# Head attention: the values matmuls of a key tile in one piece of 512 columns instead of two of 256, and another order of the matmuls around them

## The chip, the cores and the metric

One core of a Trainium2 chip runs the kernel. The metric is the device time of one execution in microseconds, taken as the median of several runs; the profile is of one further execution. TensorE (PE) does matmuls, with its weight loads shown apart as PEld; VectorE (DVE), ScalarE (ACT) and GpSimd (POOL) do the rest; SyncE (SP) issues DMAs.

## The reference, cut to what matters

The program is four layers on x of shape (2, 2048, 256): agent attention, a transformer block with a mixture of experts, a selective scan and an FP4 feed-forward. The change lies in the 16-head attention of the second layer:

```python
q = (src @ Wq + bq).reshape(B, T, NHEAD, HEAD_DIM)      # B, T = 2, 2048; 16 heads of 16
k = (src @ Wk + bk).reshape(B, T, NHEAD, HEAD_DIM)
v = (src @ Wv + bv).reshape(B, T, NHEAD, HEAD_DIM)
scores = jnp.einsum('bqhd,bkhd->bhqk', q, k) * scale
probs = jax.nn.softmax(scores, axis=-1)
out = jnp.einsum('bhqk,bkhd->bqhd', probs, v).reshape(B, T, d)
```

## The kernel before

The function `head_attention` treats four heads (a quad) and 512 queries (`GN`) as one step. There are 2 batches x 4 quads x 4 query chunks = 32 steps (`STEPS`), and each step goes over 16 key tiles of 128 keys (`KT`), so there are 512 iterations (st, kt). In each iteration TensorE has three kinds of work, and the names below are used from here on:

- **First pass** (`first_pass`, L977): four matmuls of 48 rows x 512 columns, x = 0 to 3, which give the logits of queries against keys for the row maxima. Matmuls 0 and 2 use the array's rows 0 to 63, matmuls 1 and 3 rows 64 to 127. Each writes one PSUM bank of `ps_m`, and there are three such banks (`BANKS`), taken in the fixed turn of `BankPlan`. VectorE reduces each bank to its maximum (`maxima_of`, L921), in the same order. `bank_free` makes each first-pass matmul wait until the reduce of the one three places earlier in the turn is over. The first pass runs 21 units ahead of the rest (`ahead`: one step and `LEAD` = 5).
- **Scores** (`scores`, L992): for each of two pairs of heads, two matmuls of 50 rows x 512 columns, one for each half of the array's rows, into `ps_s[pair]`. ScalarE turns them to `probs` with an Exp (`exps`, L876), 128 x 1024 each.
- **Values** (`values`, L1004): for each of four heads, probs times v into 32 partitions of `ps_o`. Each uses 128 rows and 32 columns of the array, so that the four lie side by side in it. The matmul is fp32 and is profiled as two instructions.

ScalarE's `exps(n, 0)` waits until the values of tile n - 2 are done (`pv_done`), because `probs` has room for two tiles; the scores of a pair wait until that pair's last Exp is done.

In iteration kt the order on TensorE is now: values of tile kt - 1 for the first 256 query columns; first pass 0 and 1; scores of kt + 1, pair 0; values of kt - 1 for the last 256 columns; first pass 2 and 3; scores of kt + 1, pair 1. At the end of iteration 1, `turn_out` (L1013) transposes the last step's output, and at the end of iteration 11 (`LEAD_SHIFT`) `turn_shift` (L983) transposes the next step's maxima; each takes one place in the turn of the three banks, and ScalarE copies it out (L887; L895 and L896). VectorE reduces the maxima of a step to one shift at L928.

Of the kernel before, what the change touches and what calls it, by code (L numbers as in the profile page):

```python
# [26 lines left out]
GN = GT * P  # L27
# [431 lines left out]
VW = 32  # L459
# [213 lines left out]
QC = L // GN  # L673
KT = L // P
NQ = B * QUADS
STEPS = NQ * QC
# [39 lines left out]
def ahead(st, kt):  # L716

    return (st + 1, kt + LEAD) if kt + LEAD < UNITS else (st + 2, kt + LEAD - UNITS)
# [5 lines left out]
def unit_of(i):  # L724

    return i // 8, i % 8 // 2, i % 2 * 2


def head_attention(nc, scratch, ident):
# [6 lines left out]
    with ExitStack() as ctx:  # L736
        r = Room(nc, ctx, "att")
        qs, ks = r.sb("qs", [P, 2, QC, PAIRS, GN], F32R), r.sb("ks", [P, 2, PAIRS, L], F32R)
        vs = [r.sb(f"vs{i}", [P, KT, QH * VW]) for i in range(2)]
# [4 lines left out]
        probs = r.sb("probs", [P, 4, 2, GN])  # L744
# [5 lines left out]
        ps_o = r.ps("ps_o", [P, GN])  # L750
# [5 lines left out]
        shifted, exp_done, pv_done = r.sem("shifted"), r.sem("exp_done"), r.sem("pv_done")  # L756
# [8 lines left out]
        def rows_of(e, first, n):  # L765
            return slice(e * ROW_TILE + first, e * ROW_TILE + first + n)

        with nc.Block() as block:
# [185 lines left out]
            @block.tensor  # L954
            def _(pe):

                def bank_free(key):

                    last = plan.before(key)
                    if last is None:  # L960
                        return
                    if last[0] == "shift":
                        pe.wait_ge(m_copied, 2 * (last[1] + 1))
                    elif last[0] == "out":
                        pe.wait_ge(o_t_ready, last[1] + 1)
                    else:
                        pe.wait_ge(maxed, plan.reduced[last])

                def first_pass(s, i, x):

                    key = ("m", s, i, x)
                    p, t, chunk = unit_of(i)
                    own, c = rows_of(x % 2, 0, TERMS), chunk + x // 2
                    if i == 0 and x == 0 and s % QC == 0 and s > 0:
                        pe.wait_ge(quad_loaded, s // QC * LOADS)
                    bank_free(key)
                    pe.matmul(ps_m[plan.bank(key)][:, :], qs[own, s // QC % 2, s % QC, p, t * P:(t + 1) * P],  # L977
                              ks[own, s // QC % 2, p, c * GN:(c + 1) * GN], start=True, stop=True).then_inc(scored, 1)

                def turn_shift(s):  # L980
                    bank_free(("shift", s))
                    pe.wait_ge(m_ready, s + 1)
                    pe.transpose(ps_m[plan.bank(("shift", s))][0:QT, 0:P], m_neg[:, :], ident[:, :]).then_inc(m_turned, 1)  # L983

                def scores(st, kt, pair):
                    n = st * KT + kt
                    if kt == 0 and pair == 0:
                        pe.wait_ge(shift_loaded, (st + 1) * SHIFTS)
                    if n > 0:
                        pe.wait_ge(exp_done, 2 * (n - 1) + pair + 1)  # L990
                    for e in range(2):
                        mm = pe.matmul(ps_s[pair][:, e, :], ks[rows_of(e, 0, ROWS), st // QC % 2, pair, kt * P:(kt + 1) * P],  # L992
                                       qs[rows_of(e, 0, ROWS), st // QC % 2, st % QC, pair, :], start=True, stop=True)
                    mm.then_inc(shifted, 1)

                def values(st, kt, half):

                    n = st * KT + kt
                    cols = slice(half * (GN // 2), (half + 1) * (GN // 2))
                    pe.wait_ge(exp_done, 2 * (n + 1))  # L1000
                    if kt == 0 and half == 0 and st > 0:
                        pe.wait_ge(o_copied, st)
                    for h in range(QH):
                        mm = pe.matmul(ps_o[h * VW:(h + 1) * VW, cols], vs[st // QC % 2][:, kt, h * VW:(h + 1) * VW],  # L1004
                                       probs[:, (2 * n + h // 2) % 4, h % 2, cols], start=(kt, half) == (0, 0), stop=(kt, half) == (KT - 1, 1))
                    if half == 1:
                        mm.then_inc(pv_done, 1)

                def turn_out(st):
                    bank_free(("out", st))  # L1010
                    pe.wait_ge(o_copied, st + 1)
                    for t in range(GT):
                        mm = pe.transpose(ps_m[plan.bank(("out", st))][:, t * P:(t + 1) * P], o_sb[:, t * P:(t + 1) * P], ident[:, :])  # L1013
                    mm.then_inc(o_turned, 1)

                for i in range(UNITS):
                    if i % (UNITS // 2) == 0:
                        for h in (2 * i // UNITS * 2, 2 * i // UNITS * 2 + 1):
                            pe.wait_ge(first_loaded[h], (HEAD_LOADS + (h == QH - 1)) * 16)
                    for x in range(4):  # L1020
                        first_pass(0, i, x)
                turn_shift(0)
                for i in range(LEAD):
                    for x in range(4):
                        first_pass(1, i, x)
                pe.wait_ge(ones_laid, 4 * PAIRS * 16)
                def next_scores(st, kt, pair):
                    if kt + 1 < KT:
                        scores(st, kt + 1, pair)
                    elif st + 1 < STEPS:  # L1030
                        scores(st + 1, 0, pair)

                def last_values(st, kt, half):
                    if kt > 0:
                        values(st, kt - 1, half)
                    elif st > 0:
                        values(st - 1, KT - 1, half)

                scores(0, 0, 0)
                scores(0, 0, 1)  # L1040
                for st in range(STEPS):
                    for kt in range(KT):
                        s, i = ahead(st, kt)
                        last_values(st, kt, 0)
                        if s < STEPS:
                            first_pass(s, i, 0)
                            first_pass(s, i, 1)
                        next_scores(st, kt, 0)
                        last_values(st, kt, 1)
                        if s < STEPS:  # L1050
                            first_pass(s, i, 2)
                            first_pass(s, i, 3)
                        next_scores(st, kt, 1)
                        if st > 0 and kt == 1:
                            turn_out(st - 1)
                        if st + 1 < STEPS and kt == LEAD_SHIFT:
                            turn_shift(st + 1)
                for half in range(2):
                    values(STEPS - 1, KT - 1, half)
                turn_out(STEPS - 1)  # L1060


# [1861 lines left out]
```

## Time and profile before

| | us |
|---|---|
| median of 3 runs | 3895.88 (3894.23 to 3899.1) |
| the profiled execution | 3899.1 |
| its span in the trace | 3897.4 |
| head attention's main loop, within the span | about 300 to 1640 |

The page's busy shares of the whole span are PE 85%, PEld 49%, DVE 75%, ACT 52% and POOL 30%. They mix all layers; for this change only the stretch from about 300 to 1640 us counts. A timeline row gives the start, the time from the start of the first to the end of the last instruction of a merged group, the engine, the line, the operation and the count. A matmul's row starts with its weight load when the array is not at work for it, and starts later where the load went ahead.

### The profile page before, as it was taken

Reading aid. Unit: us, or ns where it says so; the run is one execution under the profiler, and the core shown is the slowest. Engines: PE = TensorE matmul, PEld = TensorE weight load, DVE = VectorE, ACT = ScalarE, POOL = GpSimd, SP = SyncE. Lnnn points to the kernel's source line nnn. Section 1 sums busy time; section 2 is a strip of 40 time slices with the busy share of each in tenths; the row PEclk is TensorE's granted clock in tenths of the full one; section 3 lists DMA queues with packets and bytes.
Section 4 is the critical chain, followed back from the end, with each engine's and each line's share of the span. In section 5 each row is a group of like instructions: output and inputs, shape, how many; then the busy total and the mean of one; then the engine's idle time right before and its main releaser. Section 6 shows DMA issues by size and latency. Waiting matters only on the chain. (4 is left out here: it accounts for less than half of the span.)

```text
span 3897.4 us, 87366 instructions
## 1 busy us (share of the span) xinstructions
PE 3311.1 (85%) x34938; PEld 1906.6 (49%) x34939; DVE 2921.1 (75%) x4552; ACT 2033.6 (52%) x2900; POOL 1184.2 (30%) x928
## 2 busy tenths in 40 slices
PE   4769999999999999875999749984989898847876
PEld 1433333333333333254666433333867677636665
DVE  5659999999999999334444346773879798758986
ACT  0316777777777777721111255664454564325553
POOL 0100000000000000015000730002889899847775
PEclk8868999999999999966999759997999999979998
DMA  1664123030321300152221442334333333221110
GB/s 54 224 175 46 19 34 48 5 49 5 48 32 21 47 6 5 29 186 96 66 65 60 126 158 92 127 122 131 98 114 108 121 107 108 80 73 54 57 33 19
DMA packets 231409, 296.89 MB, mean 76 GB/s; under 512 B 51577, under 2 KB 166530, under 8 KB 229378
## 3 DMA queue, kind: packets, MB, share of 16 engines
q1 hardware_dynamic: 213794, 258.22, 24.2%
q0 software_dynamic: 6144, 17.05, 1.3%
q10 hardware_dynamic: 11120, 16.62, 1.2%
q8 instruction: 260, 4.26, 0.5%
q14 instruction: 91, 0.75, 0.1%
HBM read 174.75 MB, written 116.47 MB: 75 GB/s over the span
## 5 line engine op out<-in xcount | busy, mean ns | idle before, releaser
L921 DVE TENSOR_REDUCE att_maxima<-att_ps_m 128x1 f32<-128x512 f32 x2048 | 1285.6, 684 | 80.1 <-PE att_ps_m L977 78.3
L876 ACT ACTIVATE att_probs<-att_ps_s 128x1024 f32<-128x1024 f32 x1024 | 999.3, 1021 | 280.8 <-PE att_ps_o L1004 268.2
L1004 PE MATMUL att_ps_o<-att_probs,att_vs 128*32 128x256 f32 x8192 | 657.0, 393 | 4.9 <-ACT att_probs L876 0.6
L2220 POOL TENSOR_TENSOR ss_ch<-ss_h,ss_c_rep 128x1024 f32<-128x1024 f32 x256 | 602.3, 2390 | 86.8 <-DVE ss_h L2298 86.7
L977 PE MATMUL att_ps_m<-att_ks,att_qs 48*128 48x512 f32 x2048 | 584.1, 511 | 29.9 <-DMA att_ks<-scratch_k 29.2
L2328 PE MATMUL ss_ps_u<-ss_diag,ss_dx_t 128*32 128x128 f32 x16384 | 493.5, 279 | 86.3 <-DVE ss_h L2298 49.7
L2328 PEld LDWEIGHTS ss_ps_u<-ss_diag,ss_dx_t 128*32 128x32 f32 x16384 | 467.5, 113 | 146.6 <-issue 91.1
L977 PEld LDWEIGHTS att_ps_m<-att_ks,att_qs 48*128 48x128 f32 x2048 | 238.3, 188 | 472.6 <-DVE att_maxima L921 389.4
L2252 ACT ACTIVATE ss_decay<-ss_delta,ss_a_neg 128x1024 f32<-128x1024 f32 x256 | 292.0, 1146 | 335.7 <-DVE ss_h L2298 178.1
L992 PE MATMUL att_ps_s<-att_qs,att_ks 50*128 50x512 f32 x2048 | 453.8, 404 | 3.6 <-DMA att_qs<-att_m_parts 0.8
L2298 DVE TENSOR_TENSOR_SCAN ss_h<-ss_decay,ss_ps_u 128x1024 f32<-128x1024 f32 x128 | 283.8, 2270 | 96.2 <-PE ss_ps_u L2328 54.1
L1004 PEld LDWEIGHTS att_ps_o<-att_probs,att_vs 128*32 128x32 f32 x8192 | 162.5, 108 | 360.9 <-issue 339.6
L2298 DVE TENSOR_TENSOR_SCAN ss_h<-ss_decay,ss_carry,ss_ps_u 128x1024 f32<-128x1024 f32 x128 | 291.0, 2328 | 48.2 <-ACT ss_decay L2252 20.8
L992 PEld LDWEIGHTS att_ps_s<-att_qs,att_ks 50*128 50x128 f32 x2048 | 222.5, 188 | 24.7 <-ACT att_probs L876 20.8
L856 POOL TENSOR_TENSOR att_heads<-att_o_t,att_sums 128x256 f32<-128x256 f32 x32 | 19.8, 619 | 692.9 <-DVE att_sums L936 692.9
L849 POOL TENSOR_TENSOR att_m_parts<-att_m_t,att_m_parts 16x128 fp32r<-16x128 f32 x32 | 14.4, 449 | 680.3 <-ACT att_m_parts L896 680.3
L1457 ACT ACTIVATE ex_y<-ex_ps_y,ex_x 128x256 f32<-128x256 f32 x72 | 34.1, 473 | 301.7 <-PE ex_ps_y L1528 301.7
L1661 POOL DMA_INDIRECT mo_back<-scratch_sorted_y,moe_packed x64 | 61.1, 954 | 345.5 <-DMA mo_b_norm<-in_b_norm 318.7
L2035 PE MATMUL si_ps_xz<-si_xn_t,si_w_in 128*128 128x512 f32 x256 | 119.5, 622 | 35.1 <-ACT si_xp L1983 15.8
L2207 POOL TENSOR_SCALAR_AFFINE_SELECT ss_diag<-ss_b_t 128x512 f32<-128x512 f32 x64 | 40.4, 642 | 339.7 <-DMA ss_b_t<-scratch_b_t 339.7
L1510 PE MATMUL ex_ps_h<-moe_w_w,ex_x_t 128*128 x288 | 137.2, 599 | 0.4 <-issue 0.4
L1528 PE MATMUL ex_ps_y<-moe_w_w,ex_hid_t 128*128 x576 | 136.1, 379 | 0.0
(391 smaller groups left out, 4570.0 us busy)
## 6 DMA issues: line engine op xcount, KB each, us to landing
ss_delta<-scratch_delta SPq DMA_DIRECT2D x64, 512.0 KB
att_qs<-scratch_q SPq DMA_DIRECT2D x96, 128.0 KB, 9.3
att_ks<-scratch_k SPq DMA_DIRECT2D x96, 128.0 KB, 10.7
ex_x<-scratch_sorted_x SPq DMA_DIRECT2D x72, 132.0 KB, 2.1
scratch_sorted_y<-ex_y SPq DMA_DIRECT2D x72, 128.0 KB, 1.7
scratch_v<-qkv_v_ext SPq DMA_DIRECT2D x8, 1024.0 KB
scratch_q<-qkv_parts SPq DMA_DIRECT2D x16, 512.0 KB, 5.3
scratch_k<-qkv_parts SPq DMA_DIRECT2D x16, 512.0 KB, 6.0
```

What stands on the lines that cost most here:

```text
L876: act.activation(probs[:, (2 * n + pair) % 4, :, :], ps_s[pair][:, :, :], ACT.Exp, scale=HD ** -0.5).then_inc(exp_done, 1)
L921: dve.tensor_reduce(maxima[:, j, at:at + 1], ps_m[plan.bank(key)][:, :], AX.X, ALU.max).then_inc(maxed, 1)
L977: pe.matmul(ps_m[plan.bank(key)][:, :], qs[own, s // QC % 2, s % QC, p, t * P:(t + 1) * P], ks[own, s // QC % 2, p, c * GN:(c + 1) * GN], ...
L992: mm = pe.matmul(ps_s[pair][:, e, :], ks[rows_of(e, 0, ROWS), st // QC % 2, pair, kt * P:(kt + 1) * P], qs[rows_of(e, 0, ROWS), st // QC % ...
L1004: mm = pe.matmul(ps_o[h * VW:(h + 1) * VW, cols], vs[st // QC % 2][:, kt, h * VW:(h + 1) * VW], probs[:, (2 * n + h // 2) % 4, h % 2, cols ...
L1510: mm = pe.matmul(ps_h[slot][:, :], x_t[:, slot, k, :], w1[:, bass.ds(e, 1), k, :].rearrange("p a f -> p (a f)"), start=k == 0, stop=k == K ...
L1528: mm = pe.matmul(ps_y[slot][:, 0, :], hid_t[:, slot, f, :], w2[:, bass.ds(e, 1), f, :].rearrange("p a c -> p (a c)"), start=f == 0, stop=f ...
L2035: mm = pe.matmul(ps_xz[n % XZ][:, :], w_in[:, k, n * P:(n + 1) * P], xn_t[:, slot, k, :], start=k == 0, stop=k == KC - 1)
L2220: pool.tensor_tensor(ch[:, w.n % (CH_GROUPS * DQ), :], h[:, w.n % H_SLOTS, :], c_rep[:, w.ng, :], ALU.mult).then_inc(s["ch_ready"], 1)
L2252: act.activation(decay[:, w.n % DECAYS, :], delta[:, w.delta % DELTAS, :], ACT.Exp, scale=a_neg[:, at:at + 1]).then_inc(s["decay_ready"], 1)
L2298: dve.tensor_tensor_scan(h[:, w.n % H_SLOTS, :], decay[:, w.n % DECAYS, :], ps_u[w.n % U_BANKS][:, :], start, ALU.mult, ALU.add).then_inc( ...
L2328: mm = pe.matmul(ps_u[w.n % U_BANKS][q * DSUB:(q + 1) * DSUB, j * P:(j + 1) * P], dx_t[:, w.part % 2, j, w.dq * DSUB:(w.dq + 1) * DSUB], d ...
```

## The change

`values` loses its argument `half`: one matmul for each head covers all 512 query columns. The lag and lead of the work are expressed as before (values of the last tile, scores of the next), but the order changes. In iteration kt it is now: first pass 0; scores of **kt**, pair 1; first pass 1; values of kt - 1, all columns; first pass 2 and 3; scores of kt + 1, pair 0. The order of the first-pass matmuls in the turn of the banks, and everything on the other engines, stay as they are.

```diff
-                def values(st, kt, half):
+                def values(st, kt):
                     n = st * KT + kt
-                    cols = slice(half * (GN // 2), (half + 1) * (GN // 2))
                     pe.wait_ge(exp_done, 2 * (n + 1))
-                    if kt == 0 and half == 0 and st > 0:
+                    if kt == 0 and st > 0:
                         pe.wait_ge(o_copied, st)
                     for h in range(QH):
-                        mm = pe.matmul(ps_o[h * VW:(h + 1) * VW, cols], vs[st // QC % 2][:, kt, h * VW:(h + 1) * VW],
-                                       probs[:, (2 * n + h // 2) % 4, h % 2, cols], start=(kt, half) == (0, 0), stop=(kt, half) == (KT - 1, 1))
-                    if half == 1:
-                        mm.then_inc(pv_done, 1)
+                        mm = pe.matmul(ps_o[h * VW:(h + 1) * VW, :], vs[st // QC % 2][:, kt, h * VW:(h + 1) * VW],
+                                       probs[:, (2 * n + h // 2) % 4, h % 2, :], start=kt == 0, stop=kt == KT - 1)
+                    mm.then_inc(pv_done, 1)
...
                 scores(0, 0, 0)
-                scores(0, 0, 1)
                 for st in range(STEPS):
                     for kt in range(KT):
                         s, i = ahead(st, kt)
-                        last_values(st, kt, 0)
                         if s < STEPS:
                             first_pass(s, i, 0)
+                        scores(st, kt, 1)
+                        if s < STEPS:
                             first_pass(s, i, 1)
-                        next_scores(st, kt, 0)
-                        last_values(st, kt, 1)
+                        if kt > 0:
+                            values(st, kt - 1)
+                        elif st > 0:
+                            values(st - 1, KT - 1)
                         if s < STEPS:
                             first_pass(s, i, 2)
                             first_pass(s, i, 3)
-                        next_scores(st, kt, 1)
+                        if kt + 1 < KT:
+                            scores(st, kt + 1, 0)
+                        elif st + 1 < STEPS:
+                            scores(st + 1, 0, 0)
```

## Rows read from the trace of the kernel before

**Rows 1.** The page, costliest groups: line, engine, names and shapes, busy and mean, idle before

```profile
L921 DVE TENSOR_REDUCE att_maxima<-att_ps_m 128x1 f32<-128x512 f32 x2048 | 1285.6, 684 | 80.1 <-PE att_ps_m L977 78.3
L876 ACT ACTIVATE att_probs<-att_ps_s 128x1024 f32<-128x1024 f32 x1024 | 999.3, 1021 | 280.8 <-PE att_ps_o L1004 268.2
L1004 PE MATMUL att_ps_o<-att_probs,att_vs 128*32 128x256 f32 x8192 | 657.0, 393 | 4.9 <-ACT att_probs L876 0.6
```

**Rows 2.** Windows by stretch: busy us (count) of PE, PEld, DVE, ACT, POOL; clock

```profile
304.40:317.40 13.00, 13.00 (x78) 4.23 (x80) 7.70 (x13) 6.24 (x7) 0.00 (x0) 0.50 1.07 128
...
1592.00:1640.00 48.00, 44.44 (x441) 15.30 (x437) 2.57 (x6) 42.03 (x46) 1.07 (x2) 1.00 0.02 4
1000.00:1200.00 200.00, 199.33 (x1861) 77.48 (x1858) 193.33 (x316) 155.39 (x173) 4.89 (x10) 1.00 0.22 34
```

**Rows 3.** Timeline of two iterations in the steady loop

```profile
1000.39 0.64 PE L1004 MATMUL att_ps_o<-att_probs,att_vs 128*32 128x256 f32 x8
...
1002.90 0.64 PE L1004 MATMUL att_ps_o<-att_probs,att_vs 128*32 128x256 f32 x8
1003.47 0.21 PEld L977 LDWEIGHTS att_ps_m<-att_ks,att_qs 48*128 48x128 f32 x2 [0.41 <-DVE att_maxima L921]
1003.47 0.52 PE L977 MATMUL att_ps_m<-att_ks,att_qs 48*128 48x512 f32 x2
...
1003.81 0.41 PE L992 MATMUL att_ps_s<-att_qs,att_ks 50*128 50x512 f32 x2
1004.15 0.16 PEld L1004 LDWEIGHTS att_ps_o<-att_probs,att_vs 128*32 128x32 f32 x8 [0.36 <-issue]
1004.15 0.64 PE L1004 MATMUL att_ps_o<-att_probs,att_vs 128*32 128x256 f32 x8
...
1005.42 0.64 PE L1004 MATMUL att_ps_o<-att_probs,att_vs 128*32 128x256 f32 x8
```

**Rows 4.** Timeline of VectorE alone, the first step's maxima, ahead of the loop

```profile
259.71 28.78 DVE L921 TENSOR_REDUCE att_maxima<-att_ps_m 128x1 f32<-128x512 f32 x48
```

**Rows 5.** Timeline where VectorE had been idle before a reduce

```profile
1011.87 0.50 PE L977 MATMUL att_ps_m<-att_ks,att_qs 48*128 48x512 f32 x2
...
1012.40 1.29 DVE L921 TENSOR_REDUCE att_maxima<-att_ps_m 128x1 f32<-128x512 f32 x2 [0.29 <-PE att_ps_m L977]
...
1013.11 0.54 PE L977 MATMUL att_ps_m<-att_ks,att_qs 48*128 48x512 f32 x2
```

**Rows 6.** Timelines at 1.2 GHz, cut to single instructions

```profile
301.43 0.62 PE L992 MATMUL att_ps_s<-att_qs,att_ks 50*128 50x512 f32 x1
301.50 0.98 PE L977 MATMUL att_ps_m<-att_ks,att_qs 48*128 48x512 f32 x2
...
308.70 1.08 PE L1004 MATMUL att_ps_o<-att_probs,att_vs 128*32 128x256 f32 x8
310.87 0.65 PE L1004 MATMUL att_ps_o<-att_probs,att_vs 128*32 128x256 f32 x4
```

**Rows 7.** Timeline around the next step's shift

```profile
1007.85 0.22 DVE L928 TENSOR_REDUCE att_m_neg<-att_maxima 128x16 f32<-128x64 f32 x1
...
1008.10 2.48 DVE L921 TENSOR_REDUCE att_maxima<-att_ps_m 128x1 f32<-128x512 f32 x4
...
1009.52 0.28 PE L983 MATMUL att_ps_m<-all_ident,att_m_neg 128*16 128x128 f32 x1
```

**Rows 8.** The line of the shift's reduce: duration, first and last start

```profile
L928 DVE TENSOR_REDUCE att_m_neg<-att_maxima x32: 219/220/220, 288.5 to 1594.1; 128x16 f32<-128x64 f32 x32
```

**Rows 9.** Timeline around the transposes of a step's output

```profile
1024.27 0.40 PE L1004 MATMUL att_ps_o<-att_probs,att_vs 128*32 128x256 f32 x4
...
1024.60 0.53 PE L977 MATMUL att_ps_m<-att_ks,att_qs 48*128 48x512 f32 x2
...
1024.94 0.42 PE L992 MATMUL att_ps_s<-att_qs,att_ks 50*128 50x512 f32 x2
...
1025.29 0.66 PE L1013 MATMUL att_ps_m<-all_ident,att_o_sb 128*128 128x128 f32 x4
1025.87 0.16 PEld L1004 LDWEIGHTS att_ps_o<-att_probs,att_vs 128*32 128x32 f32 x8 [0.17 <-ACT att_probs L876]
```

**Rows 10.** Timeline of the last iterations, which have no first pass

```profile
1619.82 0.49 PE L992 MATMUL att_ps_s<-att_qs,att_ks 50*128 50x512 f32 x2
1619.96 1.94 ACT L876 ACTIVATE att_probs<-att_ps_s 128x1024 f32<-128x1024 f32 x2 [0.27 <-PE att_ps_o L1004]
...
1620.24 0.64 PE L1004 MATMUL att_ps_o<-att_probs,att_vs 128*32 128x256 f32 x8
1621.03 0.19 PEld L992 LDWEIGHTS att_ps_s<-att_qs,att_ks 50*128 50x128 f32 x2 [0.63 <-ACT att_probs L876]
...
1622.16 1.94 ACT L876 ACTIVATE att_probs<-att_ps_s 128x1024 f32<-128x1024 f32 x2 [0.27 <-PE att_ps_o L1004]
```

More of the change, by code:

```diff
@@ L1026, in _ @@
                 pe.wait_ge(ones_laid, 4 * PAIRS * 16)
[L1027 to L1037, printed above, removed]
                 scores(0, 0, 0)
-                scores(0, 0, 1)
                 for st in range(STEPS):
@@ L1057, in _ @@
                             turn_shift(st + 1)
-                for half in range(2):
-                    values(STEPS - 1, KT - 1, half)
+                values(STEPS - 1, KT - 1)
                 turn_out(STEPS - 1)
```

## The prediction

> **What bounds the kernel now.** I read the page first, then the windows over the attention loop, then its timeline. The page names the loop's big groups: VectorE's reduces, ScalarE's Exps, TensorE's values [rows 1]. The window says who is short of time there: of 200 us PE is busy 199.3, DVE 193.3, ACT 155.4, at a granted clock of 1.00, which is 2.4 GHz [rows 2]. ScalarE has slack; its idle time ends with a values matmul, but what it makes is needed later than it comes.
>
> TensorE and VectorE must be told apart. From one iteration's first values to the next one's are (1005.42 - 1000.39) / 2 = 2.515 us [rows 3]. VectorE can do better: ahead of the loop 48 reduces take 28.78 us, so (28.78 - 0.68) / 47 = 0.598 each and 2.39 for four [rows 4]. TensorE's half iteration is values to first pass 0.57, to scores 0.34, to values 0.34, together 1.25 [rows 3], twice that 2.50. So the loop runs at TensorE's pace.
>
> Next to it lies a loop of dependences through the three banks. A first-pass matmul sent to an idle array is followed by its reduce 0.53 later (1011.87 to 1012.40). That reduce takes 0.69, and when it ends at 1013.09 the second matmul of the pair at 1013.11 can go: the pair's 0.54 instead of 0.50 shows it 0.04 behind the first, at 1013.15, so 0.06 after the reduce's end [rows 5]. Together 0.53 + 0.69 + 0.06 = 1.28 from a first-pass matmul to the one three places on. Now that is first pass 0 to 3, or 2 to the next 1, always half an iteration apart: 1.25 by TensorE's own pace, 1.28 by the banks. The two nearly balance. What the new order puts inside this loop decides.
>
> **The change, part by part.**
>
> *Size of the values.* A set of four values instructions starts 0.24 before the next set: values to first pass is 0.57 in all [rows 3], and from the second set to the first pass 0.33 (1024.27 to 1024.60) [rows 9]. At 1.2 GHz the sets are 1.08 - 0.65 = 0.43 apart [rows 6], which is 512 cycles for 256 columns, so the columns set the time. With 512 columns I take 0.43 + 0.02 = 0.45 from set to set and 0.33 + 0.21 = 0.54 from the second set to the first pass; the bounds are 0.43 and 0.48 (twice 0.24). Half the instructions, about the same time: by itself worth nearly nothing.
>
> *Fewer turns between kinds of work.* Values to first pass leaves the array empty while weights load; scores to values does so a little. There will be one such round for each iteration instead of two. But first pass 0 and 1 are no longer side by side in the array's two halves: with the scores between them they take three places in a row (0, scores, 1) where a pair took one beside the scores. At 1.2 GHz a matmul follows the one before it on the same rows after 0.43 (scores 301.43, first pass 301.50 + 0.98 - 0.62 = 301.86) [rows 6]. At 2.4 GHz I take 0.24, bounded by 0.21 (that over two) and 0.34 (first pass to scores) [rows 3]. TensorE's own sum is then 0.45 + 0.54 + 0.34 + 3 x 0.24 + 0.34 = 2.39, and with 0.34 for the three 2.69.
>
> The Trainium skill, in TensorEngine Tiling (Array Packing), Key Properties, says that a change of tiling mode drains the engine, a change of tile alone does not. The trace agrees: 0.33 from values to first pass against 0.24 from values to values. By that rule alone the change is a gain; its time is the first rival below.
>
> *What the new order puts into the bank loop.* First pass 1 takes the bank of the last iteration's first pass 2. Between the two stand only the scores, first pass 0 and the scores. After first pass 1, and behind it in TensorE's queue, come the whole values, and then first pass 2. So the chain of one iteration is:
>
> - first pass 2 to its reduce 0.53, the reduce 0.69, its end to first pass 1 0.06 [rows 5];
> - first pass 1, sent to an idle array, to values: 0.42, as scores to values where nothing runs before them (1619.82 to 1620.24) [rows 10];
> - values, first to second set 0.45; second set to first pass 2 0.54.
>
> Sum 2.69 us, against 2.515: +0.175. First pass 1 would be sent 1.28 after first pass 2; TensorE would be free for it at about 0.34 + 3 x 0.24 = 1.06. If the three slots cost 0.34 each, it is ready at 1.36, but then overlaps its weight load and values follow after 0.34: 1.36 + 0.34 + 0.45 + 0.54 = 2.69 again. The result hardly depends on that unknown.
>
> Is VectorE ready for it? Its four reduces need 2.39, so it stands 0.3 idle before the reduce of first pass 2 and starts it on arrival. ScalarE: Exp 0 of a tile starts after scores at about 0.8, ends at 1.8; Exp 1 ends at 2.75; the scores that need them come 1.2 and 0.6 later. The waiting values need the Exp of the tile before, done long ago. No DMA is moved; SP's loads of the next quad, which wait for the values, have whole steps in hand.
>
> *The steps' ends.* A step takes now (1594.1 - 1007.85) / 14 = 41.88 [rows 7, 8], which is 16 x 2.515 + 1.64. In the new order `turn_shift` and `turn_out` each move the banks by one, so that first pass 0 of the next iteration takes the bank of the last first pass 2, and first pass 1 that of 3. For `turn_out`: first pass 2 at 0, 0's bank free at 1.28 (the four transposes, 0.93 from scores to values [rows 9] against 0.34, end about then, at 1.30), reduce of 3 over at 1.82, first pass 1 at 1.88, values 2.30, first pass 2 at 3.29: +0.60. For `turn_shift` VectorE finishes its last reduce (0.68), and the next starts 0.25 after L928's (1007.85 to 1008.10) [rows 7]: some 0.36 more than between neighbours, which its idle time takes in but for 0.08: +0.68. ScalarE's copies of the extra bank are done by 2.4, when first pass 2 at 3.3 wants it. New step: 16 x 2.69 + 1.28 = 44.32, +2.44.
>
> *The last 21 iterations* have no first pass. Now they go by Exp to scores to second values to Exp, 2.20 [rows 10]. In the new order Exp (0.92 + 1.02), 0.06, scores to values 0.42, 0.45, 0.54, scores 0.49 and 0.07 to the Exp make 3.97 for two iterations: 1.99. About 17 of them gain 0.21: -3.7.
>
> *The start.* Three iterations run at a clock of 0.50, 1.2 GHz [rows 2], at 4.32 us (twice 310.87 - 308.70 [rows 6]); one more place of 0.43 and one round of turns less (2.16 - 4 x 0.43 = 0.44) leave them as they are, 0.5 less than counted at +0.175.
>
> **Sum** against the profiled execution's 3899.1: 30 steps x 2.44 = 73.2; eleven iterations of step 30 with its `turn_out`, 11 x 0.175 - 0.2 = 1.7; start -0.5; end -3.7: +70.7, so 3969.8. The median of the runs is 3.2 lower: 3966.6, rounded to 3967.
>
> **The rivals.**
>
> *TensorE's pace (faster).* The bank wait of first pass 1 is not met or is hidden, and the loop falls to TensorE's 2.39, which is VectorE's 2.39 too. For it: the fewer turns. Against it: the bank chain of 1.28, which the split pairs show at work today. It needs a bank chain under 1.0. Per step 16 x 2.39 + 1.28 = 39.5, so -2.36 x 30 - 5 = -76: 3820. This ends on the other side.
>
> *The weight load goes ahead of the wait (faster).* First pass 1 would save 0.19 of its 0.50 and the loop is 2.50: per step -0.6, in all -22: 3874. Against it: the weight load's row starts with the matmul's, not before it, after the wait for a reduce [rows 3].
>
> *Three slots of 0.34 and nothing overlapped (slower still).* Values follow first pass 1 after 0.42 all the same: 1.36 + 0.42 + 0.45 + 0.54 = 2.77, +39 more: 4006.
>
> *The clock falls.* TensorE now stands still for some 0.2 in each iteration. At 1.2 GHz an iteration is about 4.3, so a tenth of the stage there would add 50 x 1.6 = 80: 4047. Against it: in the last 48 us, where PE waits on every Exp and is busy 44.4, the clock is 1.00 [rows 2].
>
> **How the numbers follow.** Forecast 0.77; TensorE's pace 0.06; early weight load 0.04; slots of 0.34 unhidden 0.08; clock 0.04; something that cancels within 0.2% 0.01. About 0.2% is what a measurement of this kernel can tell from no change. Faster 0.09, same 0.02, slower 0.89. The forecast's own range: 0.03 us on the chain is 15, the steps' ends another 8: 3945 to 3990. Taking in the slower slots gives 3942 to 4006.
>
> **What the profile after would show.** The values as x4096 of 128x512 with sets 0.45 apart; the iteration at 2.69; VectorE idle about 0.3 before one reduce of four, released by a first pass (today 80 us in all [rows 1], then about 200); first pass 1 alone, starting 0.06 after the end of the reduce of first pass 2 and 1.28 after that matmul's start; values 0.42 behind it; the tail at 2.0. If first pass 1 starts within 1.1 of first pass 2, or VectorE's reduces stand back to back, the prediction is wrong and the time is under 3900.

## The result, and the profile after

The changed kernel takes 3960.68 us (median of 4 runs, 3950.42 to 3965.22), the kernel before 3895.06 (4 runs, 3890.79 to 3899.1). The ratio is 1.0165, with a 95% interval of 1.0141 to 1.0188: 1.65% slower, which is small but clear of the noise, and as forecast (3967, range 3942 to 4006). The profiled execution took 3972.1 us, span 3970.4; the prediction's sum for it was 3969.8.

The page of the changed kernel, its costliest groups (they answer to [rows 1]):

```profile
L921 DVE TENSOR_REDUCE att_maxima<-att_ps_m 128x1 f32<-128x512 f32 x2048 | 1276.2, 683 | 163.1 <-PE att_ps_m L977 158.5
L876 ACT ACTIVATE att_probs<-att_ps_s 128x1024 f32<-128x1024 f32 x1024 | 998.4, 1021 | 383.4 <-PE att_ps_s L992 379.3
...
L1003 PE MATMUL att_ps_o<-att_probs,att_vs 128*32 128x512 f32 x4096 | 546.5, 606 | 0.5 <-ACT att_probs L876 0.4
```

The values are half as many instructions, and their busy time even fell, from 657 to 547 us. VectorE does the same reduces, but its idle time before them doubled, from 80 to 163 us, and a first-pass matmul ends it. Busy time went down and the kernel got slower: what counts is the waiting.

Windows of the changed kernel (columns as in [rows 2]), first in mid-loop, then at the loop's start:

```profile
1000.00:1200.00 200.00, 193.59 (x1176) 75.04 (x1176) 180.92 (x298) 145.71 (x164) 4.72 (x9) 1.00 0.18 28
...
305.00:310.00 5.00, 5.00 (x22) 2.50 (x22) 3.23 (x6) 2.73 (x3) 0.00 (x0) 0.52 0.94 116
310.00:315.00 5.00, 4.92 (x33) 1.76 (x32) 4.65 (x8) 3.88 (x4) 0.00 (x0) 1.00 1.05 128
```

Now neither TensorE nor VectorE is full: 193.6 and 180.9 of 200, where it was 199.3 and 193.3. That is how a loop of dependences looks that is longer than any engine's own work.

Timeline of one iteration of the changed kernel (against [rows 3, 5]):

```profile
1012.40 0.50 PE L977 MATMUL att_ps_m<-att_ks,att_qs 48*128 48x512 f32 x2
...
1012.74 0.40 PE L992 MATMUL att_ps_s<-att_qs,att_ks 50*128 50x512 f32 x2
...
1012.93 2.48 DVE L921 TENSOR_REDUCE att_maxima<-att_ps_m 128x1 f32<-128x512 f32 x4 [0.21 <-PE att_ps_m L977]
1012.97 0.39 PE L977 MATMUL att_ps_m<-att_ks,att_qs 48*128 48x512 f32 x1
1012.98 0.61 PE L992 MATMUL att_ps_s<-att_qs,att_ks 50*128 50x512 f32 x2
...
1013.68 0.49 PE L977 MATMUL att_ps_m<-att_ks,att_qs 48*128 48x512 f32 x1
1014.10 0.16 PEld L1003 LDWEIGHTS att_ps_o<-att_probs,att_vs 128*32 128x32 f32 x8 [0.24 <-issue]
1014.10 1.07 PE L1003 MATMUL att_ps_o<-att_probs,att_vs 128*32 128x512 f32 x8
1015.10 0.19 PEld L977 LDWEIGHTS att_ps_m<-att_ks,att_qs 48*128 48x128 f32 x2 [0.84 <-DVE att_maxima L921]
```

The chain can be read off: first pass 2 at 1012.40; its reduce at 1012.93 (+0.53); with the 0.69 of one reduce (the row shows four together) that ends at about 1013.62; first pass 1 at 1013.68, alone (+0.06), 1.28 after first pass 2; values at 1014.10 (+0.42); the next first pass 2 at 1015.10 (+1.00). An iteration is 2.70 us.

The line of the step's shift reduce in the changed kernel (against [rows 8]):

```profile
L928 DVE TENSOR_REDUCE att_m_neg<-att_maxima x32: 219/220/221, 290.7 to 1670.2; 128x16 f32<-128x64 f32 x32
```

From first to last it is 1379.5 us, before 1305.6: +73.9, and the span grew by 73.0. The whole loss is in these 31 steps, which last 44.5 us each and lasted 42.1.

### The profile page after: what moved, and what is told of

Read it like the earlier page. It is cut to its first block and busy times, and to the rows that moved or that the text cites. A ratio compares the mean times of both kernels' runs of the same rounds, so it can differ in the third digit from the quotient of the medians.

```text
span 3970.4 us, 79174 instructions
## 1 busy us (share of the span) xinstructions
PE 3342.3 (84%) x30842; PEld 1913.8 (48%) x30843; DVE 2909.7 (73%) x4552; ACT 2028.2 (51%) x2900; POOL 1184.7 (30%) x928
## 5 line engine op out<-in xcount | busy, mean ns | idle before, releaser
L977 PE MATMUL att_ps_m<-att_ks,att_qs 48*128 48x512 f32 x2048 | 743.9, 488 | 72.3 <-DMA att_ks<-scratch_k 28.9
L977 PEld LDWEIGHTS att_ps_m<-att_ks,att_qs 48*128 48x128 f32 x2048 | 300.8, 188 | 758.6 <-DVE att_maxima L921 650.2
L1003 PE MATMUL att_ps_o<-att_probs,att_vs 128*32 128x512 f32 x4096 | 546.5, 606 | 0.5 <-ACT att_probs L876 0.4
L992 PE MATMUL att_ps_s<-att_qs,att_ks 50*128 50x512 f32 x2048 | 466.0, 402 | 1.9 <-ACT att_probs L876 1.2
L992 PEld LDWEIGHTS att_ps_s<-att_qs,att_ks 50*128 50x128 f32 x2048 | 279.5, 187 | 33.1 <-ACT att_probs L876 23.6
L1003 PEld LDWEIGHTS att_ps_o<-att_probs,att_vs 128*32 128x32 f32 x4096 | 81.0, 108 | 125.8 <-issue 124.2
L2339 PE MATMUL ss_ps_y<-ss_ch,ss_sum_block 128*32 128x512 f32 x1024 | 126.0, 601 | 12.5 <-POOL ss_ch L2210 12.5
```

Of the source, the lines that this page charges most:

```text
L1003: mm = pe.matmul(ps_o[h * VW:(h + 1) * VW, :], vs[st // QC % 2][:, kt, h * VW:(h + 1) * VW], probs[:, (2 * n + h // 2) % 4, h % 2, :], sta ...
L2339: mm = pe.matmul(ps_y[dq * DSUB:(dq + 1) * DSUB, cols], block[:, :], ch[:, group % CH_GROUPS * DQ + dq, cols], start=False, stop=group % N ...
```

## The experiments

Each total is of one execution, with one execution of the kernel before on the same chip beside it (3900.4 for the first four, 3893.0 for the next three, 3908.7 for the last), except where intervals are given. The verdicts rest on the length of an iteration in each trace, which repeats to 0.01 us. Totals repeat less well: with loops alike, the layers behind the attention took 2256 us in the profiled execution of the changed kernel (3970.4 - 1714.3, the start of the last `turn_out` matmul) and 2230 in the fourth experiment's (3942.5 - 1712.5). The loop has no part in these 26 us, so a total of one execution does not decide less than about 25 us here.

### 1. A shorter reduce

```diff
-dve.tensor_reduce(..., ps_m[plan.bank(key)][:, :], AX.X, ALU.max)
+dve.tensor_reduce(..., ps_m[plan.bank(key)][:, 0:GN // 2], AX.X, ALU.max)
```

> The changed kernel with each reduce of the first pass over 256 of its bank's 512 columns: half of the keys are left out of the row maxima. Theory (the bank loop sets the iteration): the reduce falls from 0.68 to about 0.42 us, the chain from first pass 2 to first pass 1 from 1.28 to 1.02, and the iteration from 2.70 to TensorE's own 2.40 to 2.45, in all about 150 us less, near 3815. Rival (three places in a row of 0.34 make TensorE's own sum 2.69): the iteration stays at 2.65 to 2.70 and the time at 3955 to 3970.

Measured 3822.66 us. TensorE's timeline in this run:

```profile
1001.75 0.50 PE L977 MATMUL att_ps_m<-att_ks,att_qs 48*128 48x512 f32 x2
...
1002.76 0.50 PE L977 MATMUL att_ps_m<-att_ks,att_qs 48*128 48x512 f32 x1
1003.19 1.07 PE L1003 MATMUL att_ps_o<-att_probs,att_vs 128*32 128x512 f32 x8
1004.18 0.49 PE L977 MATMUL att_ps_m<-att_ks,att_qs 48*128 48x512 f32 x2
```

First pass 1 comes 1.01 after first pass 2 instead of 1.28, and the iteration is 2.43 instead of 2.70: the reduce is 0.27 shorter, the iteration too, one for one, though VectorE was never full. The rival is out. The 2.43 lies in the range that I gave, but for another reason: I took 2.40 to 2.45 for TensorE's own pace, while first pass 1 at 1002.76 still waits for the reduce (0.53 + 0.41 + 0.06 = 1.00), so the banks still set the iteration.

### 2. The order alone

```diff
+for half in range(2):
+    cols = slice(half * (GN // 2), (half + 1) * (GN // 2))
     for h in range(QH):
-        mm = pe.matmul(ps_o[h * VW:(h + 1) * VW, :], ...)
+        mm = pe.matmul(ps_o[h * VW:(h + 1) * VW, cols], ...)
```

> The new order with the values in two pieces of 256 columns, one right behind the other. Theory: the values block grows from 0.45 + 0.54 to 3 x 0.24 + 0.33 = 1.05, the iteration from 2.70 to 2.75, the time by about 28 to near 3995. Rival (the larger matmul is what costs): the iteration falls towards 2.52 and the time under 3930.

Measured 3957.91 us. TensorE's timeline:

```profile
1010.35 0.49 PE L977 MATMUL att_ps_m<-att_ks,att_qs 48*128 48x512 f32 x1
1010.77 1.07 PE L1005 MATMUL att_ps_o<-att_probs,att_vs 128*32 128x256 f32 x16
1011.77 0.50 PE L977 MATMUL att_ps_m<-att_ks,att_qs 48*128 48x512 f32 x2
...
1013.05 0.49 PE L977 MATMUL att_ps_m<-att_ks,att_qs 48*128 48x512 f32 x1
```

Both numbers missed. The iteration is 2.70, neither 2.75 nor 2.52: sixteen instructions of 256 columns take the same 1.07 us as eight of 512. Of 0.24 from a set to the next, 0.02 or 0.03 is paid once at the head of a block, not at each set. So the size of the matmuls changes nothing, and the order does all of it.

### 3. The size alone, in the order of before

```diff
+last_values(st, kt)                 # all 512 columns
 first_pass(s, i, 0); first_pass(s, i, 1)
 next_scores(st, kt, 0)
-last_values(st, kt, 1)
 first_pass(s, i, 2); first_pass(s, i, 3)
 next_scores(st, kt, 1)
```

> The order of before, with the whole values in one place at the head of the iteration, in 512 columns, then first pass 0 and 1, scores, first pass 2 and 3, scores. Theory: first pass 3 comes 1.28 after first pass 0, then scores 0.34, values 0.34, 0.45, 0.54: 2.95 an iteration, over 4080 in all. Rival (turns between kinds of work set TensorE's pace; side by side pairs are kept, one round of turns less): TensorE 2.15, VectorE 2.39, so the iteration is 2.40 and the time about 3830.

Measured 4066.52 us, the slowest with fp32 values. TensorE's rows:

```profile
1000.54 1.07 PE L1003 MATMUL att_ps_o<-att_probs,att_vs 128*32 128x512 f32 x8
...
1001.53 0.50 PE L977 MATMUL att_ps_m<-att_ks,att_qs 48*128 48x512 f32 x2
...
1002.81 0.49 PE L977 MATMUL att_ps_m<-att_ks,att_qs 48*128 48x512 f32 x1 [0.31 <-DVE att_maxima L921]
...
1003.47 1.06 PE L1003 MATMUL att_ps_o<-att_probs,att_vs 128*32 128x512 f32 x8
```

The last first pass comes 1.28 after the first pair, then scores, then values: 2.93 here and 2.95 in the next iteration (1003.47 to 1006.42), 2.94 in the mean against 2.95 worked out. The total stayed under the 4080 expected, in part because the steps' ends cost less: a step is 47.9 us, which is 16 x 2.94 and 0.8, against 1.3 in the changed kernel. Pairs side by side and one round of turns less do not help. Values in one piece lengthen the loop in both places tried; the new order, which puts the scores into the wait, is the better place for them.

### 4. First pass 0 and 1 side by side again

```diff
-first_pass(s, i, 0)
 scores(st, kt, 1)
+first_pass(s, i, 0)
 first_pass(s, i, 1)
```

> The changed kernel with the scores of pair 1 ahead of first pass 0, so that first pass 0 and 1 stand side by side again. Theory: first pass 1 still waits for the reduce of the last first pass 2, so the iteration stays at 2.69 to 2.71 and the time within 10 of the changed kernel's. Rival (single first-pass matmuls, one half of the array idle, are the cost): one place of 0.24 to 0.34 less, iteration 2.40 to 2.47, time 3830 to 3870.

Measured 3944.21 us. TensorE's timeline:

```profile
1012.63 1.06 PE L1003 MATMUL att_ps_o<-att_probs,att_vs 128*32 128x512 f32 x8
...
1014.43 0.97 PE L977 MATMUL att_ps_m<-att_ks,att_qs 48*128 48x512 f32 x2
1015.33 1.06 PE L1003 MATMUL att_ps_o<-att_probs,att_vs 128*32 128x512 f32 x8
```

Values start 2.70 apart, as in the changed kernel. First pass 0 and 1 stand side by side in the queue, but the row of 0.97 for the two shows that the second still starts about 0.48 after the first, for it waits for its bank. The time lies 16.5 below its median, outside the 10 that I gave; by the 2256 against 2230 above that is the layers behind (from the first to the last L928 the two differ by 0.5 us: 1379.0 and 1379.5). That the single matmuls cost the time is out.

### 5 and 6. A fourth bank

PSUM has no bank to spare here, so one was freed in both runs by leaving out a head's scores.

```diff
-ps_s = [r.ps(f"ps_s{i}", [P, 2, GN]) for i in range(2)]
+ps_s = [r.ps(f"ps_s{i}", [P, 2 - i, GN]) for i in range(2)]    # both runs
-BANKS = 3
+BANKS = 4                                                       # the second run
```

> The changed kernel with the fourth head of each quad left out of scores and Exp (its values are taken with the third head's probabilities), to free one PSUM bank; still three banks for the first pass. The control of the run with four banks. The scores matmul left out ran beside another, so TensorE's time stays. Both theories: iteration 2.70 while there is a first pass; the last 21 iterations shorter, since Exp of pair 1 covers 512 columns; in all 3940 to 3970.

> As the run with three heads and three banks, with the freed bank given to the first pass: four banks. Theory: first pass 1 waits for the reduce of first pass 1 of the iteration before, long over, so the bank loop is gone and the iteration falls to TensorE's and VectorE's own pace, 2.39 to 2.45; against the control 130 to 160 us less, near 3810. Rival (the order itself, with first-pass matmuls one by one, or the wait for the reduce's latency in general, costs the time): iteration 2.65 to 2.70 and less than 20 us against the control.

Measured 3979.68 and 3803.79 us. The control stayed at 2.70 (values at 1002.84, 1005.54, 1008.24), 10 over the upper end of the range in all. Its loop began with some ten iterations at 1.2 GHz (clock 0.50 from 305 to 345), and from the first to the last L928 it took 1393.1 us against 1379.5 in the changed kernel. So of the 176 us between the two runs some 14 are the control's slow start; the rest is somewhat over the 130 to 160 expected. With four banks, the timeline:

```profile
1005.73 10.83 DVE L921 TENSOR_REDUCE att_maxima<-att_ps_m 128x1 f32<-128x512 f32 x18
...
1009.28 1.06 PE L1003 MATMUL att_ps_o<-att_probs,att_vs 128*32 128x512 f32 x8
...
1011.67 1.06 PE L1003 MATMUL att_ps_o<-att_probs,att_vs 128*32 128x512 f32 x8
```

Eighteen reduces without a gap in 10.83 us, 0.597 each, and 2.39 an iteration: one bank more, and the same order runs at VectorE's pace. It is the clearest proof of the bank loop. It also shows TensorE's own pace (with one scores matmul less, which in the changed kernel runs beside another), in the iteration right behind `turn_shift`, where VectorE has a queue of full banks to work on:

```profile
1003.39 0.50 PE L977 MATMUL att_ps_m<-att_ks,att_qs 48*128 48x512 f32 x2
...
1005.51 0.19 PEld L977 LDWEIGHTS att_ps_m<-att_ks,att_qs 48*128 48x128 f32 x2 [0.84 <-DVE att_maxima L921]
```

2.12 us, not the 2.39 that I had summed.

### 7. The shorter reduce in the kernel before

The edit is that of the first experiment.

> The kernel before with each reduce of the first pass over 256 of 512 columns (half of the keys are left out of the row maxima). Theory: the iteration of before was set by TensorE's sum, 2.50, with 0.02 from the banks, so it falls from 2.515 to 2.49 to 2.50 although VectorE has 1.07 us less to do in it; with shorter steps' ends the time falls by 15 to 40, to 3860 to 3885. Rival (VectorE, busy 97% in the loop, sets it): the iteration falls well under 2.45 and the time under 3850.

Measured 3859.96 us, at the lower edge of the range (3860). Values start at 1006.24, and four half iterations later at 1011.19: 2.475 an iteration against 2.515, a little below the 2.49 to 2.50 expected. The window:

```profile
1000.00:1200.00 200.00, 199.31 (x1913) 74.71 (x1911) 120.53 (x324) 159.87 (x178) 5.37 (x10) 1.00 0.17 26
```

VectorE's busy share fell from 97% to 60%, TensorE's stayed at 199.3 of 200. The kernel before was held by TensorE, with some 0.04 from the banks; VectorE's 97% was no bound.

### 8. The new order only where there is no first pass

```diff
+if s >= STEPS:                      # the last 21 iterations
+    scores(st, kt, 1)               # (not in the first of them)
+    last_values(st, kt, 0)
+    last_values(st, kt, 1)
+    next_scores(st, kt, 0)
+    ...
+    continue
```

> The kernel before, with the new order of scores and values only in the last 21 iterations, where there is no first pass (values still in two pieces, one behind the other). Theory: these iterations fall from 2.21 to 2.00 us as they do in the changed kernel (the profile after has them at 2.00), nothing else moves: 3 to 5 us less than before, a ratio of 0.9990. Rival (the tail of the changed kernel gains from the single large values): less than 1 us.

Measured 3890.48 us (12 runs) against 3899.26 (17 runs): ratio 0.9978, interval 0.9959 to 0.9997: faster by 0.2%, with an interval that just excludes no change. Timeline of its last iterations (against [rows 10]):

```profile
1624.54 1.07 PE L1004 MATMUL att_ps_o<-att_probs,att_vs 128*32 128x256 f32 x16
...
1626.50 1.07 PE L1004 MATMUL att_ps_o<-att_probs,att_vs 128*32 128x256 f32 x16
```

1.96 here and 2.06 in the next, where it was 2.20, with values in two pieces: the gain is the order's. The profile accounts for 4 us of it; the median's 9 are within the interval. It is the only version here with all of the work in place that is not slower than the kernel before.

### 9 and 10. Values in bf16

```diff
-probs = r.sb("probs", [P, 4, 2, GN])
+probs = r.sb("probs", [P, 4, 2, GN], BF16)
+vb = [r.sb(f"vb{i}", [P, KT, QH * VW], BF16) for i in range(2)]   # rounded from vs by GpSimd
```

> The kernel before with probabilities and values in bf16, so that a values matmul is one instruction instead of two (GpSimd rounds each quad's values once). Theory: each set of values goes away that took 0.24, twice an iteration, TensorE's sum falls to about 2.02, and the iteration stops at VectorE's 2.39 or a little over it, 2.39 to 2.47 for the banks' waits; 3790 to 3865. Rival (the banks' loop of 1.28 twice, 2.56): the iteration does not fall below 2.50.

> The changed kernel with probabilities and values in bf16, values of 512 columns in one instruction for each head. Theory: the chain of one iteration loses the second set, 1.28 + 0.42 + 0.33 = 2.03, so VectorE's 2.39 becomes the bound: 16 x 0.3 = 4.9 us a step less than in the changed kernel, 3790 to 3830, and equal to or below the order of before in bf16. Rival (the single first-pass matmuls or the bank wait cost more than the chain says): over 2.50 an iteration.

Measured 4157.49 us, ratio 1.0657 (1.0628 to 1.0687), and 4056.28 us, ratio 1.0412 (1.0384 to 1.0440). Both are more than 200 us above the ranges that I gave. The window of each, in mid-loop:

```profile
600.00:1000.00 400.00, 400.00 (x2070) 174.10 (x2068) 329.58 (x524) 268.61 (x286) 12.22 (x18) 0.50 0.17 25
```

```profile
600.00:1000.00 400.00, 400.00 (x1669) 215.00 (x1670) 341.87 (x560) 276.05 (x306) 12.93 (x20) 0.50 0.18 25
```

The granted clock is 0.50, 1.2 GHz, in the whole loop, where the kernel before and the changed one have 1.00 from about 318 and 310 us on. In TensorE's own work the values are all that changed; why the clock stays low with them no run shows. So these runs can't say what the chain does at 2.4 GHz; that stays open. At 1.2 GHz the new order is the faster one: an iteration is 2.85 us (values at 951.75 and 954.60) where the order of before has 3.06 (950.71 and 953.77), and 101 us less in all. TensorE is busy 400 of 400 us in both, so it sets the pace there and not the banks.

### 11. Four banks in the order of before

The edits are those of the fourth-bank run, on the kernel before.

> The kernel before, old order and values in two pieces, with the fourth head of each quad left out of scores and Exp (its values are taken with the third head's probabilities) and four banks for the first pass. Theory: TensorE's own sum with two rounds of turns keeps the iteration at 2.48 to 2.50, where the new order with four banks has 2.39: the new order gains with four banks what it loses with three. Rival (any order falls to VectorE's pace once a bank is spare): 2.39 to 2.42.

TensorE's timeline:

```profile
902.12 0.64 PE L1004 MATMUL att_ps_o<-att_probs,att_vs 128*32 128x256 f32 x8
...
903.35 0.64 PE L1004 MATMUL att_ps_o<-att_probs,att_vs 128*32 128x256 f32 x8
...
904.59 0.64 PE L1004 MATMUL att_ps_o<-att_probs,att_vs 128*32 128x256 f32 x8
```

The iteration is 2.47, a little under the 2.48 to 2.50 stated and above the rival's 2.39 to 2.42. It is TensorE's pace with two rounds of turns: the short reduce in the kernel before leaves the same 2.475 with VectorE at 60%. The total, 3977.15 us, says nothing on the orders, for the clock was at 0.50 in stretches of this run, up to about 450 us and again in the second window below:

```profile
600.00:1000.00 400.00, 398.56 (x3669) 150.10 (x3668) 392.17 (x649) 251.43 (x355) 10.70 (x20) 1.00 0.18 26
1070.00:1170.00 100.00, 100.00 (x532) 33.21 (x535) 58.90 (x95) 38.00 (x51) 1.69 (x3) 0.50 0.02 4
```

| iteration, us at 2.4 GHz | order of before | new order |
|---|---|---|
| three banks | 2.515 | 2.70 |
| three banks, short reduce | 2.475 | 2.43 |
| four banks (three heads) | 2.47 | 2.39 |

## Why the prediction was right, point by point

- **What bounds before: TensorE, not VectorE.** Right: the short reduce moved it by 0.04 only. TensorE's own pace is 2.47 rather than 2.50; the 0.04 above it are the banks' waits.
- **Size of the values: nearly nothing.** Right in the sum (values block 1.00, worked out 0.99), and the order-alone run shows it outright. Its two parts were each off by 0.02 or 0.03 and cancelled: from the first set to the second 0.43 (1.07 less the 0.64 of one set), not 0.45, and from the second set to first pass 2 0.57, not 0.54. The upper bound of 0.48 per set was not needed: doubling 0.24 counted its fixed part twice.
- **The bank loop, 2.69.** Measured 2.70. Its links stand in the timeline within 0.01 (0.53, 0.06, 0.42 and the 1.00 of the values). VectorE stands idle 0.21 in each iteration, not 0.3, since its four reduces take 2.48 when they wait for banks; hence 163 us in all and not 200. The short reduce, the size-alone run and the fourth bank moved it by 0.27, 0.24 and 0.31, each in the direction that the loop gives and to within 0.01 where a size follows from it.
- **TensorE's own sum, 2.39.** Wrong size: measured 2.12, in one iteration of the four-bank run. I gave first pass 0, scores and first pass 1 three places of 0.24. They take two: in the timeline after, first pass 0 at 1012.97 and one scores matmul at 1012.98 start together, the other follows at 1013.20. A first-pass matmul fills only one half of the array's rows, and the scores matmul of the other half runs beside it. The bank loop stood above either sum, so the forecast did not suffer. The first rival's time was right only because VectorE's 2.39 would have held it. With four banks the old order takes TensorE 2.47 and the new one 2.12 (VectorE then holds it at 2.39), so one round of turns between values and the rest is worth 0.35. The Trainium skill's rule in TensorEngine Tiling (Array Packing), Key Properties, that a change of tiling mode drains the engine, agrees with that; by that rule alone the change would have been a gain, and with a fourth bank it is.
- **The steps' ends, 1.28.** 31 steps of 44.5 less 16 x 2.70 = 43.2 leave 1.3. Values to values is 3.37 over `turn_shift` (1002.64 to 1006.01) and 3.30 over `turn_out` (1019.50 to 1022.80), so +0.67 and +0.60 where +0.68 and +0.60 were worked out.
- **The last iterations, -3.7.** From the last L928 to the last `turn_out` matmul 47.7 us before (1594.1 to 1641.8), 44.1 after (1670.2 to 1714.3): -3.6.
- **The start.** The clock rose to 1.00 at about 310 us instead of 318, so there was about one slow iteration in the changed kernel, not three. This hid a miss, and that was luck. In VectorE's timelines the second L928 stands at 336.48 before and at 335.34 after. From the first to the second the changed kernel took 3.3 less, where the sum for the start and the eleven odd iterations had 1.2 more. The 30 steps from there on grew by 77.3 (1257.65 to 1334.9), where the sum had 73.2, mostly because 2.70 stands for 2.69 in 480 iterations. The two misses of 4 nearly cancel in the 73.9. Whether the order or chance raised the clock earlier, no run shows. The loop's first L928 came 2.2 later, in work that the change does not touch.
- **The clock.** The rival with a chance of 0.04 did not come, but the bf16 runs and the eleventh show that it was nearer than the window of the last iterations made it seem: with the values in bf16 the clock never rises in the loop.

Over all 73.9 + 2.2 - 3.6 + 0.5 (all that lies behind) = 73.0. The median moved by 65.6; the difference of 7 to the profiled execution is of the size of the 26 us by which the later layers vary between executions.

## What to carry to other kernels

Where an engine waits in order, a large block of work put behind the wait adds its full length to the chain of dependences: find the chain from producer to consumer and back through the last free buffer, and add what the queue holds behind it. Two buffer waits of 1.28 us, each with half of the block in between, were nearly free; one wait with the whole block behind it cost 0.18 us in 2.5. And an order can't be judged apart from its number of buffers: with four banks (and three heads' scores) the new order is the faster one, with three the slower.

## What the runs showed of the hardware beyond that

- Matmuls on different halves of the array's rows overlap even when they are not issued as a pair. In the changed kernel first pass 0 and one of the two scores matmuls behind it started 0.01 apart, the other scores matmul 0.23 later, so that first pass, scores pair and first pass took two places of about 0.23 and not three. They need not even start in program order. In the four-bank run, where the program has first pass 0, one scores matmul on rows 0 to 63, and first pass 1 on rows 64 to 127, both first passes start first:

```profile
1003.96 0.39 PE L977 MATMUL att_ps_m<-att_ks,att_qs 48*128 48x512 f32 x2
...
1004.20 0.39 PE L992 MATMUL att_ps_s<-att_qs,att_ks 50*128 50x512 f32 x1
```

- The granted clock stayed at 0.50 for a whole stage of 1300 us in which the profile has PE busy 100%, when the values matmuls became bf16. In the eleventh run it was 0.50 up to about 450 us, then 1.00, 0.50 from about 1060 to 1190 and 1.00 again, with PE busy 100% from 1060 to 1180. Ahead of the fall TensorE had stood still once, for 1.92 us, until the shift's DMA landed; the scores behind that wait already take 0.80 for the pair instead of 0.40:

```profile
1058.52 0.80 PE L992 MATMUL att_ps_s<-att_qs,att_ks 50*128 50x512 f32 x2 [1.92 <-DMA att_qs<-att_m_parts]
```

  One short wait can stand ahead of some 130 us at half the clock, and a busy PE in the profile does not promise that the clock comes back.
- Back-to-back sets of four 32-column fp32 matmuls of 256 columns cost the same as half as many of 512 columns: 1.07 us each way.
